# Merging 24 instead of 11 dense blocks behind the last scatter: a predicated copy with its mask in PSUM, and stores from ScalarE's queue

## The chip, the cores and the metric

The kernel runs as one program on one core of a Trainium2 chip. The metric is the device time of one execution in microseconds (us), as the median of some executions. It is a hand-placed program: five engines (TensorE or PE, VectorE or DVE, ScalarE or ACT, GpSimd or POOL, SyncE or SP) each run a list of instructions in a fixed order and meet only at semaphores. SP and ACT can each issue plain DMA transfers from a queue of their own; POOL issues the indirect ones (gathers and scatters by a list of row numbers).

## What is computed

Four graph layers over 100,000 nodes of 64 features, with 25,000 edges. Only nodes that an edge touches get a message. Cut to what matters here:

```python
edge_index = jnp.stack([src, dst])
x = _layernorm(x + _L0_gnn_ref(x, edge_attr_16, src, dst, ...), axis=-1)
x = _layernorm(x + _L1_gnn_ref(x, edge_index, edge_weight, ...), axis=-1)   # attention, layernorm, MLP, layernorm
x = _layernorm(x + _L2_gnn_ref(x, edge_index, ...), axis=-1)
x = _layernorm(x + _L3_gnn_ref(x, src, dst, edge_weight, 100000), axis=-1)
return x                                                                    # (100000, 64) float32
```

A node without edges goes through the same norms and the MLP of layer 1, with constants in place of the messages. That is the dense part. A node with edges needs gathers, softmax and segment sums. That is the sparse part.

## The kernel before

**Dense part.** The 100,000 rows are cut into 98 blocks of 1024 rows (the last one is shifted back to end at row 100,000 and so overlaps the one before). Each block is a chain on PE, ACT and DVE in one of three lanes, and its result, 128 partitions x 512 floats (256 KB), is stored by SP (`dense_sp`). The result is right for the nodes without edges alone.

**Sparse part.** The edges stand in 25 groups of 8 columns of 125. POOL walks five long rows of indirect transfers, 200 each in 25 groups of 8: the gathers of `x` by source and by target, the gathers from `x0tab`, the scatters to `stab`, the gathers from `x2tab` and from `x3tab`. At the end it scatters the final rows of touched nodes to `out`: first 200 of kind "only" (nodes that are targets), then 200 of kind "src". These 400 are the final scatters.

**Why blocks are late.** A dense row of a touched node must not land on top of the scattered one. So POOL waits, ahead of its first final scatter, until every dense block below number `LATE0` is stored in `out`. The last `LATE` blocks (11 of them, numbers 87 to 97) go to a scratch table `late_tab` instead, and may be computed while POOL scatters. Their rows of `out` were filled beforehand with a value that can't be a result, 3e38 (`unset_sp`, on SP). At the end they are merged: once the last scatter has landed, SP loads each late block's rows of `out` (256 KB); a row that still begins with 3e38 was not scattered and takes the dense value, any other keeps the scattered one; then the block is stored. Before, `late_dve` does that with three DVE instructions a block, a mask from the first column and two `tensor_tensor` over 128x512:

```python
nc.vector.tensor_scalar(m, o[:, :, 0], UNSET / 2, UNSET, ALU.is_lt, ALU.mult)   # 3e38 where the row was scattered
nc.vector.tensor_tensor(d, d, bc(m, D), ALU.add)                                # so the dense row becomes huge there
nc.vector.tensor_tensor(o, o, d, ALU.min)                                       # and the smaller one is kept
```

The last block is stored behind all the others, since it overlaps its neighbour.

**What sets the order.** `make_plan` lays all steps of all units out by a greedy list of costs and due times before the program is written, and `play` writes each engine's steps in the order of those times. The late steps (`late_sp`, `late_dve`) have the due time 1e6, so they stand last on their engines. In the plan, the only thing that depends on `LATE` is the row of final scatters, on which nothing else depends. POOL's own list is written in plain loops.

Names in the steps: `late_d` are the dense blocks loaded back from `late_tab`, `late_o` the rows loaded from `out`, `late_m` the masks; `wk` and `u` are large work buffers (`rr` is `u` seen as rows of 136 floats), `b_gl`, `b_h`, `b_s`, `b_x1` the lanes' buffers.

Of the kernel before, what the change touches and what calls it, by code (L numbers as in the profile page):

```python
# [5 lines left out]
i32 = mybir.dt.int32  # L6
# [5 lines left out]
def gnn_resnorm_kernel(nc, x, src, dst, edge_attr, edge_weight, W1, W2, attn, bias0, W_phys, W_neur, att_w,  # L12
# [23 lines left out]
    KEY2 = 0x3F000000 >> 15  # L36
    BIGK, BIGC = 400000.0, 100000.0
    GROUPS = range(NG)
    LATE = 11
    LATE0 = NBLK - LATE  # L40
    UNSET = 3e38
    NONE = 8
# [14 lines left out]
    with ctx:  # L57
# [5 lines left out]
        def S(name):  # L63
            if name not in names:
                names[name] = ctx.enter_context(nc.semaphore(name))
            return names[name]
# [80 lines left out]
        neg2 = sb("neg2", [1, 2])  # L147
        unset = sb("unset", [128, D])
        mask8 = sb("mask8", [128, GC])
        late_d = w_[0:LATE]  # L150
        late_o = [b_gl[k % NL][:, 512 * (k // NL):512 * (k // NL) + 512] for k in range(2 * NL)] + b_h + b_s
        late_m = b_x1[0][:, 0:GC * LATE]
        ps = ctx.enter_context(nc.psum_tensor("ps", [128, 8 * 512], fp32))

        def bank(j, n=1):
            return ps[:, 512 * j:512 * (j + n)]

        pA, pB, pAB = ([bank(2 * l) for l in LANES], [bank(2 * l + 1) for l in LANES], [bank(2 * l, 2) for l in LANES])
        e0, e1 = bank(6), bank(7)

        def col(v, n=128):
            return vec[0:n, v:v + 1]
# [4 lines left out]
        def t3(a, c=GC):  # L167
            return a.rearrange("p (c d) -> p c d", c=c)
# [597 lines left out]
            tab, row = (out, dense_row(n)) if n < LATE0 else (late_tab, NB * (n - LATE0))  # L766
            sp.dma_start(tab[row:row + NB, :].rearrange("(p t) d -> p (t d)", p=128), b_gl[l][:, 0:512]).then_inc(S(f"rows_st{l}"), 16)

        FIRST_FOUND = 6
        LATE_LOADS = [LATE - 1, LATE - 2] + list(range(LATE - 2))  # L770
        LATE_STORES = [LATE - 2] + list(range(LATE - 2)) + [LATE - 1]

        def late_rows(j):
            return out[dense_row(LATE0 + j):dense_row(LATE0 + j) + NB, :].rearrange("(p t) d -> p t d", p=128)

        def unset_sp(sp, t, j):
# [3 lines left out]
                sp.wait_ge(S("late_dma"), 16 * (LATE - 1))  # L780
            sp.dma_start(late_rows(j), unset[:, :].unsqueeze(1).broadcast_to((128, GC, D))).then_inc(S("late_dma"), 16)

        def late_sp(sp, t):
            yield t
            sp.wait_ge(S("summed"), 4 * NG)
            for l in LANES:
                sp.wait_ge(S(f"rows_st{l}"), 16 * before(l, len(lane_jobs[l]), dense=1, src=1))
            sp.wait_ge(S("late_dma"), 16 * LATE)
            for j in range(LATE):
                sp.dma_start(late_d[j], late_tab[NB * j:NB * j + NB, :].rearrange("(p t) d -> p (t d)", p=128)).then_inc(S("late_dma"), 16)  # L790
            sp.wait_ge(S("final_st"), 256 * NG)
            for k, j in enumerate(LATE_LOADS):
                sp.dma_start(t3(late_o[j]), late_rows(j)).then_inc(S(f"late_found{int(k >= FIRST_FOUND)}"), 16)
            sp.wait_ge(S("late_found0"), 16 * FIRST_FOUND)
            for k, j in enumerate(LATE_STORES):
                sp.wait_ge(S("late_step"), 3 * k + 3)
                if k == LATE - 1:
                    sp.wait_ge(S("late_dma"), 32 * LATE + 16 * k)
                sp.dma_start(late_rows(j), t3(late_o[j])).then_inc(S("late_dma"), 16)
            sp.wait_ge(S("late_dma"), 48 * LATE)  # L800

        def late_dve(dve, t):
            yield t
            dve.wait_ge(S("late_dma"), 32 * LATE)
            for k, j in enumerate(LATE_STORES):
                m, d, o = late_m[:, GC * j:GC * j + GC], t3(late_d[j]), t3(late_o[j])
                second = LATE_LOADS.index(j) >= FIRST_FOUND
                dve.wait_ge(S(f"late_found{int(second)}"), 16 * (LATE - FIRST_FOUND if second else FIRST_FOUND))
                nc.vector.tensor_scalar(m, o[:, :, 0], UNSET / 2, UNSET, ALU.is_lt, ALU.mult).then_inc(S("late_step"), 1)  # L809
                dve.wait_ge(S("late_step"), 3 * k + 1)  # L810
                nc.vector.tensor_tensor(d, d, bc(m, D), ALU.add).then_inc(S("late_step"), 1)
                dve.wait_ge(S("late_step"), 3 * k + 2)
                nc.vector.tensor_tensor(o, o, d, ALU.min).then_inc(S("late_step"), 1)

# [246 lines left out]
        def l0_pe(pe, t, g):  # L1063
            yield t["xt"]
            pe.wait_ge(*gathered(0, g))
            pe.wait_ge(S("e0_free"), use("e0", t["xt"]))
            for q in range(Q):
                last_t = nc.tensor.transpose(e0[:, P * q:P * q + P], xs[0:P, GC * g + 2 * q:GC * g + 2 * q + 2, :], ident[0:P, 0:P])
            last_t.then_inc(S("l0_t"), 1)
            yield t["et"]  # L1070
            pe.wait_ge(S(f"ea_in{g % 2}"), 32 * (g // 2 + 1))
            pe.wait_ge(S("e0_free"), use("e0", t["et"]))
            nc.tensor.transpose(e0[:, 0:P], ea_t[g % 2][0:P, :], ident[0:P, 0:P]).then_inc(S("l0_et"), 1)
            yield t["f"]
            pe.wait_ge(S("e0_free"), use("e0", t["et"]) + 1)
            pe.wait_ge(S("e1_free"), use("e1", t["f"]))
            if g == 0:
                pe.wait_ge(S("w_e_in"), 16 * GC)
            nc.tensor.matmul(e1[:, 0:EW], wt[:, W1X, :], e_a[:, 0:EW], start=True, stop=False)
            for q in range(Q):  # L1080
                last_f = nc.tensor.matmul(e1[:, P * q:P * q + P], w_e[:, q, :], e_b[:, 0:P], start=False, stop=(q == Q - 1))
            last_f.then_inc(S("l0_f"), 1)
            yield t["s"]
            pe.wait_ge(S("l0_leaky"), g + 1)
            pe.wait_ge(S("e0_free"), use("e0", t["s"]))
            for q in range(Q):
                last_s = nc.tensor.matmul(e0[0:P, 2 * q:2 * q + 2], e_d[:, P * q:P * q + P], att[:, 0, :], start=True, stop=True)
            last_s.then_inc(S("l0_s"), 1)
# [1249 lines left out]
        def setup_sp(sp):  # L2338
            yield 41
            sp.wait_ge(S("w1e_t"), 1)  # L2340
            for c in range(GC):
                sp.dma_start(w_e[DE * c:DE * c + DE, c // 2, 64 * (c % 2):64 * (c % 2) + 64], w1e_t[0:DE, :]).then_inc(
                    S("w_e_in"), 16)
            yield 44
            sp.wait_ge(S("w_made"), 1)
            sp.dma_start(x0tab[E:E + 128 * NONE, :].rearrange("(p s) d -> p s d", s=NONE),
                         rowc[:, R_B0, :].unsqueeze(1).broadcast_to((128, NONE, D))).then_inc(
                S("x0_none"), 16)

        def signs_dve(dve):  # L2350
            step = [0]
# [16 lines left out]
        @block.sync  # L2368
        def _(sp):
            sp_programs = [index_sp(sp), setup_sp(sp)]  # L2370
            sp_programs += [lists_sp(sp, t0, k, (dlist, slist)[k]) for k, t0 in LISTS]
            sp_programs += lanes(sp, dense_sp, src_sp, dst_sp)
            sp_programs += [l0_sp(sp, at["l0", g], g) for g in GROUPS]
            sp_programs += [prep2_sp(sp, at["prep2", k], k) for k in range(2)]
            sp_programs += [carry_sp(sp, at["lay", layer], layer) for layer in range(4)]
            sp_programs += [edges_sp(sp, n, dlist if n < 2 * NG else slist, t0) for n, t0 in EDGES]
            sp_programs += [main0_sp(sp, n, t0) for n, t0 in MAIN[0]] + [main2_sp(sp, n, t0) for n, t0 in MAIN[1]]
            sp_programs += [rload_sp(sp, at["rl", g], g) for g in GROUPS]
            sp_programs += [unset_sp(sp, at["u3", 0]["t"] + 20 * j, j) for j in range(LATE)]
            sp_programs += [late_sp(sp, 1e6)]  # L2380
            play(*sp_programs)

        @block.gpsimd
        def _(pool):
# [40 lines left out]

            for k in range(2):
                pool.wait_ge(S(f"x0_st{k}"), 32 * ((NG + 1 - k) // 2))
            pool.wait_ge(S("x0_none"), 16)
            pool.wait_ge(S("xd_sum"), NG)
            pool.wait_ge(S("prep2_done"), 1)  # L2430
            pool.sem_inc(S("pool_turn"))
# [37 lines left out]
            for kind, g in FINAL:  # L2469
                pool.wait_ge(S("only_rows" if kind == "only" else "src_rows"), g + 1)  # L2470
                pool.sem_inc(S("pool_turn"))
                for k in range(GC):
                    b = GC * g + k
                    if kind == "src":
                        rows, ix = rsrc[:, b, :], sfin_i
                    else:
                        rows, ix = rdst[:, b, :] if g >= STAGED else staged(g)[:, D * k:D * k + D], fidx_i
                    scatter(out, last_node, ix[:, b:b + 1], rows, S("final_st"))

        @block.tensor  # L2480
        def _(pe):
# [12 lines left out]
        def _(act):  # L2494
# [5 lines left out]
            act_programs += [main_act(act, n, t0) for part in MAIN for n, t0 in part]  # L2500
            act_programs += [xd1_act(act, at["xd1", g], g) for g in GROUPS] + [x1s_act(act, at["x1s", g], g) for g in GROUPS]
            act_programs += [main2_act(act, n, t0) for n, t0 in MAIN[1]] + [main3_act(act, n, t0) for n, t0 in MAIN[2]]
            play(*act_programs)

        @block.vector
# [70 lines left out]
```

## Time and profile before

| | |
|---|---|
| median of 3 runs (lowest to highest) | 2683.65 us (2670.19 to 2685.36) |
| profiled execution: its time, its span | 2680.65 us, 2678.8 us |
| busy: PE, DVE, ACT, POOL | 1807.6, 1724.8, 1465.7, 1679.7 us |
| last scatter issued, last instruction of SP starts | 2649.43 us, 2676.40 us |

The span runs from the first to the last instruction that the profiler recorded; the execution's own time is 1.85 us more. All positions below are in us from the span's start. In rows of the timeline the first number is the start, the second the time from the start of the first to the end of the last of the merged instructions; the bracket is the idle time of the engine ahead of it and what ended that. A DMA issue (SPq, ACTq) is the time on the queue that issues it, not that of the transfer.

### The profile page before, as it was taken

The numbers are of one execution on the slowest core, as the hardware profiler recorded it, in microseconds if no ns is written. First come the engines' busy times: TensorE is split into PE (matmuls) and PEld (weight loads), VectorE is DVE, ScalarE is ACT, GpSimd is POOL, SyncE is SP. The second block draws the span as 40 slices with busy tenths as digits, with TensorE's granted clock in tenths as the row PEclk, the third lists the DMA queues.
The fourth block names the chain that finished last, engine by engine and source line by source line (L and its number), as shares of the span: only waits on it lengthen the run. The fifth ranks groups of instructions, "written<-read, shape, count | busy, mean of one in ns | idle before, by whom it ended". The sixth has DMA issues, their size and how long they took to land. (4 is left out here: it accounts for less than half of the span.)

```text
span 2678.8 us, 24741 instructions
## 1 busy us (share of the span) xinstructions
PE 1807.6 (67%) x7450; PEld 868.5 (32%) x7450; DVE 1724.8 (64%) x3305; ACT 1465.7 (55%) x2212; POOL 1679.7 (63%) x1610
## 2 busy tenths in 40 slices
PE   5999989767977888898999876568877654000000
PEld 3444444324533333344444324433322343000000
DVE  5888989988888787765555469887666775000002
ACT  3787777753676667677777755357777521000000
POOL 5777777710057771006777578775777787777774
PEclk9999999987997888899999986679999755555555
DMA  3333222214622221124444644432121233000002
GB/s 68 73 75 80 68 72 64 63 31 126 192 77 49 60 55 32 47 77 113 138 129 135 179 150 124 117 78 65 58 58 54 86 106 110 16 18 21 22 21 99
DMA packets 236808, 214.81 MB, mean 80 GB/s; under 512 B 157822, under 2 KB 170965, under 8 KB 236677
## 3 DMA queue, kind: packets, MB, share of 16 engines
q1 hardware_dynamic: 182228, 166.60, 21.7%
q0 software_dynamic: 51200, 46.31, 7.2%
q8 instruction: 60, 0.98, 0.2%
q10 hardware_dynamic: 3248, 0.34, 0.1%
q14 instruction: 72, 0.58, 0.1%
HBM read 140.36 MB, written 86.31 MB: 85 GB/s over the span
## 5 line engine op out<-in xcount | busy, mean ns | idle before, releaser
L2405 POOL DMA_INDIRECT stab<-wk,rank_i x200 | 215.0, 1075 | 267.4 <-DVE wk L621 209.1
L578 ACT ACTIVATE b_s<-ps,vec 128x512 f32<-128x512 f32 (+1 forms) x356 | 240.8, 682 | 137.7 <-PE ps L572 45.0
L2402 POOL DMA_INDIRECT e_bc<-x0tab,dpos_i x136 | 137.7, 1013 | 245.7 <-DMA x0tab<-e_bc 200.6
L2402 POOL DMA_INDIRECT u<-x2tab,dpos_i x200 | 227.8, 1139 | 80.2 <-issue 75.3
L809 DVE TENSOR_SCALAR b_x<-b_s 128x8 f32<-128x8 f32 x2 | 0.3, 167 | 396.4 <-DMA b_gl<-out_dram 396.4
L2402 POOL DMA_INDIRECT u<-x3tab,src_i x200 | 206.1, 1030 | 78.8 <-issue 59.4
L2402 POOL DMA_INDIRECT u<-in_x_dram,src_i x200 | 201.7, 1009 | 76.7 <-issue 56.9
L2402 POOL DMA_INDIRECT u<-in_x_dram,dst_i x200 | 207.7, 1038 | 64.3 <-issue 60.9
L2405 POOL DMA_INDIRECT out_dram<-u,sfin_i x200 | 196.5, 982 | 66.3 <-issue 66.3
L2405 POOL DMA_INDIRECT out_dram<-u,dst_i x176 | 197.2, 1120 | 60.6 <-issue 56.0
L566 PE MATMUL ps<-b_h,blk_c 128*128 128x512 f32 (+1 forms) x296 | 169.3, 655 | 35.6 <-ACT b_gl L586 35.1
L561 PE MATMUL ps<-b_h,wt 64*128 64x512 f32 (+1 forms) x296 | 168.4, 654 | 31.4 <-DVE b_x L720 28.5
L1029 PE MATMUL ps<-wk 127*64 127x125 f32 x1200 | 122.1, 370 | 98.3 <-DVE wk L1014 95.0
L572 PE MATMUL ps<-b_s,blk_j 128*128 128x512 f32 (+1 forms) x296 | 158.1, 621 | 34.7 <-ACT b_s L591 34.6
L575 PE MATMUL ps<-b_h,wt 128*128 128x512 f32 (+1 forms) x296 | 165.3, 649 | 15.0 <-DVE b_h L599 14.2
L586 ACT ACTIVATE b_gl<-ps,vec 128x1024 f32<-128x1024 f32 (+1 forms) x148 | 162.7, 1106 | 19.9 <-PE ps L562 18.3
L562 PE MATMUL ps<-b_h,wt 64*128 64x512 f32 (+1 forms) x296 | 168.4, 654 | 0.0
L586 ACT ACT_TABLE_LOAD x124 | 159.1, 1283 | 12.8 <-DMA out_dram<-b_gl 9.3
L567 PE MATMUL ps<-b_gl,w2c 128*64 128x512 f32 (+1 forms) x296 | 163.2, 634 | 0.0
L568 PE MATMUL ps<-b_gl,w2c 128*64 128x512 f32 (+1 forms) x296 | 163.2, 634 | 0.0
L657 PE MATMUL ps<-b_s,blk_j 128*128 128x512 f32 x240 | 136.4, 656 | 19.9 <-ACT b_s L699 11.6
L591 ACT ACTIVATE b_s<-ps,vec 128x512 f32<-128x512 f32 (+1 forms) x148 | 100.5, 679 | 84.4 <-PE ps L568 84.4
(423 smaller groups left out, 4747.4 us busy)
## 6 DMA issues: line engine op xcount, KB each, us to landing
b_gl<-in_x_dram SPq DMA_DIRECT2D x98, 256.0 KB, 2.8
wk<-dlist SPq DMA_DIRECT2D x50, 500.0 KB
wk<-slist SPq DMA_DIRECT2D x50, 500.0 KB
out_dram<-b_gl SPq DMA_DIRECT2D x93, 256.0 KB, 2.0
u<-stab SPq DMA_DIRECT2D x25, 510.0 KB
x2none<-b_gl SPq DMA_DIRECT2D x25, 250.0 KB
x0tab<-e_bc SPq DMA_DIRECT2D x25, 240.0 KB
wk<-x2none SPq DMA_DIRECT2D x25, 240.0 KB
```

Of the source, the lines that this page charges most:

```text
L561: nc.tensor.matmul(pA[l][:, 0:w], wt[0:64, W1T, :], b_h[l][0:64, 0:w], start=True, stop=True)
L562: nc.tensor.matmul(pB[l][:, 0:w], wt[64:128, W1T, :], b_h[l][64:128, 0:w], start=True, stop=True).then_inc(S(f"mlp_pe{l}"), 1)
L566: nc.tensor.matmul(pA[l][:, 0:w], blk_c[:, :], b_h[l][:, 0:w], start=True, stop=False)
L567: nc.tensor.matmul(pA[l][0:64, 0:w], w2c[:, :], b_gl[l][:, 0:w], start=False, stop=True)
L568: nc.tensor.matmul(pA[l][64:128, 0:w], w2c[:, :], b_gl[l][:, 512:512 + w], start=False, stop=True).then_inc(S(f"mlp_pe{l}"), 1)
L572: nc.tensor.matmul(pB[l][:, 0:w], blk_j[:, :], b_s[l][:, 0:w], start=True, stop=True).then_inc(S(f"means{l}"), 1)
L575: nc.tensor.matmul(pA[l][:, 0:w], wt[:, DG2, :], b_h[l][:, 0:w], start=True, stop=True).then_inc(S(f"mlp_pe{l}"), 1)
L578: return nc.scalar.activation(b_s[l][:, 0:w], pB[l][:, 0:w], ACT.Abs_reciprocal_sqrt, bias=col(EPSV))
L586: nc.scalar.activation(b_gl[l][:, :].rearrange("p (b f) -> p b f", b=2)[:, :, 0:w], pAB[l].rearrange("p (b f) -> p b f", b=2)[:, :, 0:w], ...
L657: nc.tensor.matmul(pB[l], blk_j[:, :], b_s[l][:, :], start=True, stop=True).then_inc(S(f"means{l}"), 1)
L2402: pool.indirect_dma_start(out=o, out_offset=None, in_=tab, in_offset=at_ix(ix), **kw).then_inc(s, 16)
L2405: pool.indirect_dma_start(out=tab, out_offset=at_ix(ix), in_=a, in_offset=None, bounds_check=last, oob_is_err=False).then_inc(s, 16)
```

## The change

It makes these edits:

- `LATE` is 24: blocks 74 to 97 are late. 13 more blocks go to `late_tab`, are filled with 3e38 beforehand, are loaded twice and are stored at the end. The fills are due every 12 instead of every 20 us.
- The merge of a block is two DVE instructions: a mask (1 where the first column is still 3e38), written to PSUM, and one `copy_predicated` over 128x512 that copies the dense value onto the loaded rows where the mask is set.
- `late_d` lies in the part of `u` that the "only" scatters read, in pieces of 64 floats. So its 24 loads wait for these 200 scatters, which count on a semaphore of their own (`only_st`). Before, the 11 loads went to `wk` and waited for no scatter.
- The loads of `out` rows go in chunks of three, and each chunk waits for the landing of the chunk two ahead of it (two semaphores in turn). Before, all 11 were issued in a row.
- The stores of merged blocks are issued by ACT (`late_act`) instead of SP.
- The store that fills `x0tab`'s spare rows counts on `w_e_in` instead of on a semaphore of its own; so PE waits for it too ahead of the first `w_e` matmul.

```diff
-    LATE = 11
+    LATE = 24
...
-        late_d = w_[0:LATE]
-        late_o = [b_gl[k % NL][:, 512 * (k // NL):512 * (k // NL) + 512] for k in range(2 * NL)] + b_h + b_s
-        late_m = b_x1[0][:, 0:GC * LATE]
+        late_d = [rr[:, GC * k:GC * k + GC, 0:D] for k in range(LATE)]
+        late_o = [t[:, 512 * k:512 * k + 512] for k in range(2) for t in b_gl] + b_h + b_s + b_x1 + w_
...
+        late_m = bank(0)[:, 0:GC * LATE]
...
-        FIRST_FOUND = 6
+        FOUND = 3
...
+        def late_found(k):
+            c = k // FOUND
+            in_chunk = min(FOUND, LATE - FOUND * c)
+            return S(f"late_found{c % 2}"), 16 * (FOUND * (c // 2) + in_chunk)
...
             sp.wait_ge(S("late_dma"), 16 * LATE)
+            sp.wait_ge(S("only_st"), 128 * NG)
             for j in range(LATE):
-                sp.dma_start(late_d[j], late_tab[NB * j:NB * j + NB, :].rearrange("(p t) d -> p (t d)", p=128)).then_inc(S("late_dma"), 16)
-            sp.wait_ge(S("final_st"), 256 * NG)
+                sp.dma_start(late_d[j], late_tab[NB * j:NB * j + NB, :].rearrange("(p t) d -> p t d", p=128)).then_inc(S("late_dma"), 16)
+            sp.wait_ge(S("final_st"), 128 * NG)
             for k, j in enumerate(LATE_LOADS):
-                sp.dma_start(t3(late_o[j]), late_rows(j)).then_inc(S(f"late_found{int(k >= FIRST_FOUND)}"), 16)
-            sp.wait_ge(S("late_found0"), 16 * FIRST_FOUND)
+                if k % FOUND == 0 and k >= 2 * FOUND:
+                    sp.wait_ge(*late_found(k - 2 * FOUND))
+                sp.dma_start(t3(late_o[j]), late_rows(j)).then_inc(late_found(k)[0], 16)
+
+        def late_act(act, t):
+            yield t
             for k, j in enumerate(LATE_STORES):
-                sp.wait_ge(S("late_step"), 3 * k + 3)
+                act.wait_ge(S("late_step"), 2 * k + 2)
                 if k == LATE - 1:
-                    sp.wait_ge(S("late_dma"), 32 * LATE + 16 * k)
-                sp.dma_start(late_rows(j), t3(late_o[j])).then_inc(S("late_dma"), 16)
-            sp.wait_ge(S("late_dma"), 48 * LATE)
+                    act.wait_ge(S("late_dma"), 32 * LATE + 16 * k)
+                act.dma_start(late_rows(j), t3(late_o[j])).then_inc(S("late_dma"), 16)
+            act.wait_ge(S("late_dma"), 48 * LATE)
...
-                nc.vector.tensor_scalar(m, o[:, :, 0], UNSET / 2, UNSET, ALU.is_lt, ALU.mult).then_inc(S("late_step"), 1)
-                dve.wait_ge(S("late_step"), 3 * k + 1)
-                nc.vector.tensor_tensor(d, d, bc(m, D), ALU.add).then_inc(S("late_step"), 1)
-                dve.wait_ge(S("late_step"), 3 * k + 2)
-                nc.vector.tensor_tensor(o, o, d, ALU.min).then_inc(S("late_step"), 1)
+                m, o = late_m[:, GC * j:GC * j + GC], t3(late_o[j])
+                dve.wait_ge(*late_found(LATE_LOADS.index(j)))
+                if k == 0:
+                    dve.wait_ge(*late_found(0))
+                nc.vector.tensor_scalar(m, o[:, :, 0], UNSET / 2, None, ALU.is_ge).then_inc(S("late_step"), 1)
+                dve.wait_ge(S("late_step"), 2 * k + 1)
+                nc.vector.copy_predicated(o, m.bitcast(i32).unsqueeze(2).broadcast_to((128, GC, D)), late_d[j]).then_inc(
+                    S("late_step"), 1)
...
             if g == 0:
-                pe.wait_ge(S("w_e_in"), 16 * GC)
+                pe.wait_ge(S("w_e_in"), 16 * GC + 16)
...
-            sp_programs += [unset_sp(sp, at["u3", 0]["t"] + 20 * j, j) for j in range(LATE)]
+            sp_programs += [unset_sp(sp, at["u3", 0]["t"] + 12 * j, j) for j in range(LATE)]
...
-                    scatter(out, last_node, ix[:, b:b + 1], rows, S("final_st"))
+                    scatter(out, last_node, ix[:, b:b + 1], rows, S("only_st" if kind == "only" else "final_st"))
...
+            act_programs += [late_act(act, 1e6)]
```

PE's list is the same instruction by instruction. ACT's is the same up to the 24 stores at its end, DVE's up to the merge, POOL's but for the semaphores. What differs stands in the following places.

DVE, the first two blocks of the merge, at the end of its list, before:

```order
L809 TENSOR_SCALAR b_x10<-b_s0 128x8 [waits late_found0,late_dma]
L811 TENSOR_TENSOR wk<-wk,b_x10 128x512 [waits late_step]
L813 TENSOR_TENSOR b_s0<-b_s0,wk 128x512 [waits late_step]
L809 TENSOR_SCALAR b_x10<-b_gl0 128x8 [waits late_found0]
L811 TENSOR_TENSOR wk<-wk,b_x10 128x512 [waits late_step]
L813 TENSOR_TENSOR b_gl0<-b_gl0,wk 128x512 [waits late_step]
```

and after (the first three blocks; `ps` is PSUM):

```order
L820 TENSOR_SCALAR ps<-wk 128x8 [waits late_found0,late_dma]
L822 COPY_PREDICATED wk<-ps,u 128x512 [waits late_step]
L820 TENSOR_SCALAR ps<-b_gl0 128x8 [waits late_found0]
L822 COPY_PREDICATED b_gl0<-ps,u 128x512 [waits late_step]
L820 TENSOR_SCALAR ps<-b_gl1 128x8 [waits late_found1]
L822 COPY_PREDICATED b_gl1<-ps,u 128x512 [waits late_step]
```

Three instructions a block for 11 blocks have become two a block for 24.

SP, its loads and stores at the end of its list, before (from the eighth load on):

```order
L793 DMA b_gl2<-out_0_dram 128x512
L793 DMA b_h0<-out_0_dram 128x512
L793 DMA b_h1<-out_0_dram 128x512
L793 DMA b_h2<-out_0_dram 128x512
L799 DMA out_0_dram<-b_s0 128x512 [waits late_step,late_found0]
L799 DMA out_0_dram<-b_gl0 128x512 [waits late_step]
L799 DMA out_0_dram<-b_gl1 128x512 [waits late_step]
```

and after (the loads from `late_tab`, and the first ten from `out`):

```order
L796 DMA u<-late_tab 128x8x64 [waits rows_st2,late_dma,rows_st1,only_st,rows_st0,summed]
L796 DMA u<-late_tab 128x8x64 x23
L801 DMA wk<-out_0_dram 128x512 [waits final_st]
L801 DMA wk<-out_0_dram 128x512
L801 DMA b_gl0<-out_0_dram 128x512
L801 DMA b_gl1<-out_0_dram 128x512
L801 DMA b_gl2<-out_0_dram 128x512
L801 DMA b_gl0<-out_0_dram 128x512
L801 DMA b_gl1<-out_0_dram 128x512 [waits late_found0]
L801 DMA b_gl2<-out_0_dram 128x512
L801 DMA b_h0<-out_0_dram 128x512
L801 DMA b_h1<-out_0_dram 128x512 [waits late_found1]
```

A chunk's first load now waits for an earlier chunk, and the stores have left this list: they stand at the end of ACT's.

SP during the gathers from `x0tab`, where the fills stand between the dense and `x2none` stores, before:

```order
L781 DMA out_0_dram<-unset 1024x1x64 [waits pool_c]
L767 DMA out_0_dram<-b_gl0 128x512 [waits rows_out0]
L781 DMA out_0_dram<-unset 1024x1x64 [waits pool_c]
L767 DMA out_0_dram<-b_gl1 128x512 [waits rows_out1]
L781 DMA out_0_dram<-unset 1024x1x64 [waits pool_c]
L885 DMA x2none<-b_gl1 125x512 [waits rows_out1]
```

and after:

```order
L767 DMA out_0_dram<-b_gl0 128x512 [waits rows_out0]
L781 DMA out_0_dram<-unset 1024x1x64 [waits pool_c] x2
L767 DMA out_0_dram<-b_gl1 128x512 [waits rows_out1]
L781 DMA out_0_dram<-unset 1024x1x64 [waits pool_c] x2
L895 DMA x2none<-b_gl1 125x512 [waits rows_out1]
```

The stores between which the fills stand keep their order; two fills in a row stand where one stood.

## Rows read from the trace of the kernel before

**Rows 1.** The page, part 4: the chain that ended last, by engine.

```profile
POOL 16%; issue 6%; ACT 4%; DVE 4%; PE 4%; DMA 1%; SPq 0%; POOLq 0%; ACTq 0%; DVEq 0%
```

**Rows 2.** Waits of POOL at the final scatters: us in total, times, longest.

```profile
POOL out_dram L2405 <- issue: 129.7, 399, 3.0
POOL out_dram L2405 <- DVE u L1662: 4.6, 1, 4.6
```

**Rows 3.** Timeline of POOL, last gather and first final scatter.

```profile
2096.40 1.00 POOL L2402 DMA_INDIRECT u<-x3tab,src_i  x1 [0.31 <-issue]
2097.70 1.02 POOL L2405 DMA_INDIRECT out_dram<-e_bc,dst_i  x1 [0.30 <-issue]
```

**Rows 4.** Timeline of SP, last early block's store and first late ones.

```profile
2015.84 0.34 SPq L767 DMA_DIRECT2D out_dram<-b_gl  x1
...
2027.79 6.35 SPq L767 DMA_DIRECT2D late_tab<-b_gl  x2
```

**Rows 5.** Timeline of all engines from the last scatter on.

```profile
2649.43 0.98 POOL L2405 DMA_INDIRECT out_dram<-u,sfin_i  x1 [0.30 <-issue]
2651.62 0.81 SPq L793 DMA_DIRECT2D b_s<-out_dram  x2
...
2658.87 0.17 DVE L809 TENSOR_SCALAR b_x<-b_s 128x8 f32<-128x8 f32 x1 [396.39 <-DMA b_gl<-out_dram]
2659.08 0.69 DVE L811 TENSOR_TENSOR wk<-wk,b_x 128x512 f32<-128x512 f32 x1
2659.80 0.69 DVE L813 TENSOR_TENSOR b_s<-b_s,wk 128x512 f32<-128x512 f32 x1
2660.41 0.17 DVE L809 TENSOR_SCALAR b_x<-b_gl 128x8 f32<-128x8 f32 x1
...
2675.14 0.69 DVE L813 TENSOR_TENSOR b_s<-b_s,wk 128x512 f32<-128x512 f32 x1
2676.40 0.33 SPq L799 DMA_DIRECT2D out_dram<-b_s  x1
```

**Rows 6.** Windows: length, PE, PEld, DVE, ACT, POOL (instructions), PEclk, DMA share, GB/s.

```profile
2652.00:2654.00 2.00, 0.00 (x0) 0.00 (x0) 0.00 (x0) 0.00 (x0) 0.00 (x0) 0.50 0.70 204
2654.00:2656.00 2.00, 0.00 (x0) 0.00 (x0) 0.00 (x0) 0.00 (x0) 0.00 (x0) 0.50 0.81 223
2656.00:2658.00 2.00, 0.00 (x0) 0.00 (x0) 0.00 (x0) 0.00 (x0) 0.00 (x0) 0.50 1.01 381
2658.00:2660.00 2.00, 0.00 (x0) 0.00 (x0) 1.06 (x3) 0.00 (x0) 0.00 (x0) 0.50 1.05 403
...
2666.00:2668.00 2.00, 0.00 (x0) 0.00 (x0) 1.93 (x4) 0.00 (x0) 0.00 (x0) 0.50 0.59 221
```

**Rows 7.** Wait of SP for the other stores, ahead of the last one.

```profile
SPq L798 <- DMA out_dram<-b_h: 1.7, 1, 1.7
```

**Rows 8.** The longest kind of DVE instruction between 2100 and 2260.

```profile
L1014 DVE TENSOR_TENSOR wk<-wk,vcs 127x1000 f32<-127x1000 f32 x25 | 29.7, 1190 | 0.0
```

**Rows 9.** ACT's DMA issues at the start: ns each, min/median/max.

```profile
L2269 ACTq DMA_DIRECT2D vec<-in_L_gnn_ln_g_dram x4: 617/618/618, 15.2 to 18.5; - x4
```

**Rows 10.** Window in the gathers from `x2tab`; columns as in rows 6.

```profile
1540.00:1550.00 10.00, 8.32 (x27) 2.91 (x26) 4.05 (x6) 7.56 (x10) 7.86 (x8) 1.00 0.98 262
```

**Rows 11.** The fills: timeline of one and of a gather behind it.

```profile
752.43 0.61 SPq L781 DMA_DIRECT2D out_dram<-unset  x1
...
757.12 1.35 POOL L2402 DMA_INDIRECT e_bc<-x0tab,dpos_i  x1 [0.30 <-issue]
```

**Rows 12.** Store to `x0tab`'s spare rows, and PE's first matmul of the waiting step.

```profile
37.02 0.62 SPq L2346 DMA_DIRECT2D x0tab<-rowc  x1
...
47.17 1.00 PE L1079 MATMUL ps<-e_a,wt 128*128 128x500 f32 x2
```

**Rows 13.** The page, part 6: DMA issues, KB each, median us to landing.

```profile
out_dram<-unset SPq DMA_DIRECT2D x11, 256.0 KB, 4.9
...
x0tab<-rowc SPq DMA_DIRECT2D x1, 256.0 KB, 3.4
```

More of the change, by code:

```diff
@@ L805, in late_dve @@
             for k, j in enumerate(LATE_STORES):
-                m, d, o = late_m[:, GC * j:GC * j + GC], t3(late_d[j]), t3(late_o[j])
-                second = LATE_LOADS.index(j) >= FIRST_FOUND
-                dve.wait_ge(S(f"late_found{int(second)}"), 16 * (LATE - FIRST_FOUND if second else FIRST_FOUND))
-                nc.vector.tensor_scalar(m, o[:, :, 0], UNSET / 2, UNSET, ALU.is_lt, ALU.mult).then_inc(S("late_step"), 1)
-                dve.wait_ge(S("late_step"), 3 * k + 1)
-                nc.vector.tensor_tensor(d, d, bc(m, D), ALU.add).then_inc(S("late_step"), 1)
-                dve.wait_ge(S("late_step"), 3 * k + 2)
-                nc.vector.tensor_tensor(o, o, d, ALU.min).then_inc(S("late_step"), 1)
+                m, o = late_m[:, GC * j:GC * j + GC], t3(late_o[j])
[6 more added lines that the diff above has]
+                    S("late_step"), 1)
         def src_pe(pe, l, m, t, g):
@@ L2347, in setup_sp @@
                          rowc[:, R_B0, :].unsqueeze(1).broadcast_to((128, NONE, D))).then_inc(
-                S("x0_none"), 16)
+                S("w_e_in"), 16)
         def signs_dve(dve):
@@ L2427, in _ @@
                 pool.wait_ge(S(f"x0_st{k}"), 32 * ((NG + 1 - k) // 2))
-            pool.wait_ge(S("x0_none"), 16)
+            pool.wait_ge(S("w_e_in"), 16 * GC + 16)
             pool.wait_ge(S("xd_sum"), NG)
```

## The prediction

> **What bounds the kernel now.** I read the chain that ended last first. POOL has the largest share of it, and the "issue" beside it is mostly POOL's time between two of its own instructions [rows 1]. Then POOL's waits at the final scatters. The reader is to see that it waits for others only once, 4.6 us for DVE; the other 399 idle pieces are 0.3 us each between two issues, or 3.0 at most [rows 2]. Then the start of this stretch, since that is what late blocks are for. The last gather starts at 2096.40, takes 1.00, and the first final scatter starts at 2097.70, after the usual 0.30 us [rows 3]. So POOL did not wait for a dense block. The store of the last early block had been issued at 2015.84, and the first late one at 2027.79 [rows 4]: block 86 is in `out` some 80 us before POOL asks for it. Last, the tail. The last scatter is issued at 2649.43, the first load at 2651.62, the merge runs on DVE from 2658.87 to 2675.83, the last store is issued at 2676.40 [rows 5], and the span ends at 2678.8. From the last scatter's start that is 29.4 us in which nothing but the merge runs. This tail alone is exposed; everything ahead of it from 2097 on is POOL's row of 400 scatters.
>
> **What 13 more late blocks free: nothing.** PE's list is unchanged, and so are ACT's and DVE's up to the merge; no compute moves. What moves earlier is the point from which POOL may scatter, and POOL waits there 0.30 us, as between any two [rows 3]. The 4.6 us [rows 2] end with a DVE instruction of layer 3, which doesn't depend on dense blocks. So the gain is 0; its upper bound is those 4.6 us.
>
> **The tail, by its DMA.** A block is 0.262 MB. 24 blocks loaded and stored are 24 x 2 x 0.262 = 12.58 MB; before, 11 blocks were 5.77 MB. The loads start slowly: 204 and 223 GB/s in the first four microseconds, so 0.85 MB by 2656 [rows 6]. Then the engines are full: 381 GB/s at a share of 1.01 and 403 at 1.05, so 377 to 384 GB/s at a full share; with stores alone it is 221 at 0.59, or 375 [rows 6]. I take 377 for loads and stores mixed, since both kinds alone give about that. The remaining 11.73 MB then take 31.1 us, until 2687.1. Behind that stands what can't overlap: the last store waits for the landing of all others, 1.7 us [rows 7], and from its issue to the end of the span it is 2678.8 - 2676.40 = 2.4 us [rows 5]; its own 0.7 us of transfer are in the bytes already. So the span would end at 2687.1 + 1.7 + 2.4 - 0.7 = 2690.5, which is **11.7 us later**. The bounds: with 403 GB/s throughout, 29.1 instead of 31.1, so +9.7; at the 262 GB/s that a share of 0.98 moves where gathers with short rows are among the traffic [rows 10], 44.8, so +25.4. The transfers of the tail are 2 KB pieces like those of before, so I stay near the first.
>
> The Trainium skill (DMA: Bandwidth & Descriptors, "Where 436 GB/s comes from") has HBM bind such transfers at about 358 GB/s a core. The row with 403 GB/s speaks against it over two microseconds at least. By that figure the transfers would take 32.8 us and the sum be 1.7 us more.
>
> **DVE in the tail.** Before, a block takes 2659.08 - 2658.87 = 0.21 us for the mask's place, 0.72 for the first `tensor_tensor` and 0.61 for the second [rows 5]; 11 x 1.54 = 16.9. No row shows a `copy_predicated`. If it is like the second `tensor_tensor`, 0.69 busy, a block takes 0.21 + 0.61 = 0.82 and 24 take 19.7 us. Its two bounds: less than 0.69 changes nothing, since the DMA's 31.1 are longer; the longest DVE instruction nearby, 1000 elements, takes 1.19 [rows 8], which makes 0.5 more a block, 31.7 us in all and within 1 us of the DMA. I take 0.69, by the shape. So the cheaper merge is hidden under the transfers; it decides from 31.1 / 24 = 1.3 us a block on.
>
> **ACT's stores.** A DMA issue on ACT took 0.62 us at the start of the kernel [rows 9]: 24 are 14.9 us, beside DVE and DMA, so 0. The queue matters in one way: behind a load that waits for its chunk, SP would hold back stores; on ACT they go as soon as DVE is done. ACT has nothing else left to do, so nobody waits behind them.
>
> **The chunk gate** is an added wait on SP. Queued behind it are only further loads; DVE and ACT wait for those. Before, six loads had landed 2658.87 - 2651.62 = 7.25 us after the first issue [rows 5]. Two chunks are six loads. If six in flight always took 7.25 us, a chunk would pass every 3.6 us, less than the 3.9 us that its 1.57 MB of loads and stores need at 377 GB/s (31.1 / 8). So the gate costs 0 to 2 us, inside the rounding of the sum.
>
> **The loads from `late_tab`** now start only after the 200 "only" scatters. The last 200 scatters at 0.98 + 0.30 us each take some 257 us, so these loads can be issued from about 2392. In the worst case each takes the 4.9 us of a fill, which also moves 256 KB in pieces of 64 floats [rows 13]: 118 us, over before 2520, against a need at 2652. Hidden, 130 us to spare. Do they slow POOL? In a window with DMA at 0.98, POOL still issued 8 gathers in 10 us at 0.98 us each [rows 10]. So 0.
>
> **13 more fills.** They cost SP 0.61 us each [rows 11], 8 us in all on a queue that has gaps there, and put 13 times 0.26 MB more on the DMA. The gather shown behind a fill took 1.35 us [rows 11], against 1.00 for an undisturbed one [rows 3]. If each added fill slowed one gather by 0.35, that would be 4.6 us on POOL, upstream of the end. Whether the fill did it the row doesn't tell, and DMA at 0.98 didn't slow POOL elsewhere [rows 10], so I take 1 us of 0 to 4.6. The last fill waits for the others; behind it on SP stands an `x2none` store that frees a lane, at most one landing, 4.9 us [rows 13], late, and as before.
>
> **The moved semaphore.** PE now waits for the `x0tab` store too. It is issued at 37.02 and lands 3.4 us later [rows 12, 13]; PE starts the step at 47.17 [rows 12]. Six microseconds to spare: 0.
>
> **The sum.** 2680.65 (the profiled execution) + 11.7 + 1 = **2693 us**. The runs shown have a median of 2683.65 and reach from 2670.19 to 2685.36; the profiled one lies 3 us under the median, and a median of three may be off by 5 or so. A change of under 1% (27 us) can't be told from none here, and 12 us is 0.4%.
>
> **Rivals.**
> (a) *Loads and stores don't share a limit*, and the tail goes at DVE's pace. The first chunk lands at about 2656, 19.7 us of DVE follow, then 3.0 us as before from DVE's end to the span's: 2678.7, no change, 2681 us with the fills. For it: stores come from another queue. Against it: it needs 11.7 MB in 20 us, 590 GB/s, and no window passes 403 [rows 6]. Chance 0.10. The Trainium skill (DMA: Bandwidth & Descriptors, "Issuing engines are not separate DMA queues") says that DMAs issued by different engines end up on the same 16; by it, (a) is out and the sum above stands.
> (b) *The chunk gate becomes the bound*, slower than before by over 1%. If stores that alternate with loads double the landing of a window of loads, so that a single chunk passes per 7.25 us, eight chunks take 58 us from 2651.6; three blocks of DVE and the 3.0 us at the end make 2715, so +36, 2717 us. For it: only six loads may be in flight, and the store queue fills as fast as the load queue. Against it: the engines would be idle half the time with work queued, while at 1.01 share they were not. It decides from (2705.6 - 2651.6 - 5.5) / 8 = 6.1 us a chunk. Chance 0.12.
> (c) *`copy_predicated` is twice as dear*, 1.38: 1.51 a block, 36.2 us from 2656, and 3.0: 2695, so 2698 us with the fills. Or the 262 GB/s of above: 2707. Together 0.10.
> (d) *The change does what it is made for*: in other executions POOL does wait for a dense block, and now doesn't. The 80 us between block 86's store and POOL's asking [rows 4] speak against it; a gain of over 1% would need the body to shrink by 39 us. 2654 us. Chance 0.03.
>
> **How the numbers follow.** 0.65 for the forecast with its own range 2687 to 2701. The range goes from 2679, which takes in (a), to 2711, which takes in (c); it leaves out (b) and (d), 0.15. Faster by over 1%: (d), 0.03. Slower by over 1%, past 2710.5: (b) and a corner of (c), 0.14. Within 1%: the rest, 0.83.
>
> **What would show it.** In the changed kernel's profile the first final scatter should stand 0.3 us behind the last gather, at 2097 to 2102; the last scatter at 2649 to 2655; the first `out` load 2.2 us behind it. In the tail the DMA share should be near 1.0 at about 380 GB/s for some 30 us, DVE busy for under two thirds of it and waiting for DMA, and the span's end 40 to 43 us behind the last scatter's start. `copy_predicated` should read 0.6 to 0.8 us. The loads from `late_tab` should be through by 2520 at the latest, with scatters at 0.98 beside them. I am wrong if the share in the tail stays at 0.5 to 0.7 (then the gate or DVE holds it, (b) or (c)), if the windows pass 450 GB/s (then (a)), or if POOL's row begins earlier or runs slower.

## The result, and the profile after

| | before | changed |
|---|---|---|
| median of 20 runs (lowest to highest) | 2682.47 us (2670.19 to 2688.83) | 2687.89 us (2679.70 to 2700.00) |
| ratio to before, 95% interval | | 1.0029 (1.0015 to 1.0042) |
| profiled execution's span | 2678.8 us | 2698.3 us |
| start of the last scatter | 2649.43 | 2658.56 |
| tail: from there to the span's end | 29.4 us | 39.7 us |

The change makes the kernel slower by 0.29%, 7.8 us (4 to 11); the two medians lie 5.4 us apart. The predicted direction holds. Of the forecast 12.7 us, 11.7 were for the tail and 1 for the fills; the tail grew by 10.3, and the whole change lies below the forecast by more than its interval allows. The profiled execution happened to be the slowest of the 20, so its span says less than the ratio; its tail can be read apart from that.

First the place where more late blocks could have helped. POOL's timeline of the changed kernel, last gather and first final scatter, answers to [rows 3]:

```profile
2105.86 1.00 POOL L2412 DMA_INDIRECT u<-x3tab,src_i  x1 [0.30 <-issue]
2107.16 1.02 POOL L2415 DMA_INDIRECT out_dram<-e_bc,dst_i  x1 [0.30 <-issue]
```

The gap is 0.30 us, as it was. Nothing was waited for there before, so nothing was won. Then the tail, the timeline of all engines, to be held against [rows 5]:

```profile
2658.56 0.98 POOL L2415 DMA_INDIRECT out_dram<-u,sfin_i  x1 [0.31 <-issue]
...
2660.75 0.83 SPq L801 DMA_DIRECT2D wk<-out_dram  x2
2661.62 4.84 SPq L801 DMA_DIRECT2D b_gl<-out_dram  x6
2665.76 0.17 DVE L820 TENSOR_SCALAR ps<-wk 128x8 f32<-128x8 f32 x1 [391.55 <-DMA b_gl<-out_dram]
2665.97 0.72 DVE L822 COPY_PREDICATED wk<-ps,u 128x512 f32<-128x512 int32 x1
...
2666.60 0.17 DVE L820 TENSOR_SCALAR ps<-b_gl 128x8 f32<-128x8 f32 x1
2666.73 0.36 ACTq L809 DMA_DIRECT2D out_dram<-wk  x1
...
2679.26 0.17 DVE L820 TENSOR_SCALAR ps<-b_s 128x8 f32<-128x8 f32 x1 [2.15 <-DMA b_x<-out_dram]
...
2683.84 0.17 DVE L820 TENSOR_SCALAR ps<-b_x 128x8 f32<-128x8 f32 x1 [1.98 <-DMA wk<-out_dram]
...
2686.47 9.70 ACTq L809 DMA_DIRECT2D out_dram<-wk  x8
...
2693.75 0.73 DVE L822 COPY_PREDICATED wk<-ps,u 128x512 f32<-128x512 int32 x1
```

A block starts 0.84 us behind the one before it (2666.60 - 2665.76), of which the predicated copy is 0.72. And DVE idles again and again for a load, up to 2.15 us: a reader should look at the brackets, which name a DMA each time. What the DMA did meanwhile is in the windows of the changed kernel (columns as in [rows 6]):

```profile
2662.00:2664.00 2.00, 0.00 (x0) 0.00 (x0) 0.00 (x0) 0.00 (x0) 0.00 (x0) 0.50 0.85 294
2664.00:2666.00 2.00, 0.00 (x0) 0.00 (x0) 0.20 (x2) 0.00 (x0) 0.00 (x0) 0.50 0.82 294
2666.00:2668.00 2.00, 0.00 (x0) 0.00 (x0) 1.79 (x5) 0.00 (x0) 0.00 (x0) 0.50 1.02 334
2668.00:2670.00 2.00, 0.00 (x0) 0.00 (x0) 1.93 (x5) 0.00 (x0) 0.00 (x0) 0.50 0.95 309
2670.00:2672.00 2.00, 0.00 (x0) 0.00 (x0) 1.13 (x4) 0.00 (x0) 0.00 (x0) 0.50 1.04 393
...
2678.00:2680.00 2.00, 0.00 (x0) 0.00 (x0) 0.71 (x2) 0.00 (x0) 0.00 (x0) 0.50 1.05 402
...
2690.00:2692.00 2.00, 0.00 (x0) 0.00 (x0) 1.16 (x4) 0.00 (x0) 0.00 (x0) 0.50 1.06 409
2692.00:2694.00 2.00, 0.00 (x0) 0.00 (x0) 1.90 (x6) 0.00 (x0) 0.00 (x0) 0.50 0.75 283
```

From 2670 to 2692 all engines are full, share 1.04 to 1.06, with loads and stores mixed at 389 to 409 GB/s. Before, the same share was reached for four microseconds [rows 6], and from 2662 on DVE, busy 1.90 to 1.93 of every 2 us, left the DMA at 0.35 to 0.59. Two of those windows of the kernel before:

```profile
2662.00:2664.00 2.00, 0.00 (x0) 0.00 (x0) 1.90 (x6) 0.00 (x0) 0.00 (x0) 0.50 0.42 156
...
2670.00:2672.00 2.00, 0.00 (x0) 0.00 (x0) 1.93 (x4) 0.00 (x0) 0.00 (x0) 0.50 0.35 131
```

The bound of the tail has moved from DVE to the DMA.

The loads from `late_tab`, now beside the "src" scatters. SP's timeline and a window of all engines:

```profile
2400.69 26.17 SPq L796 DMA_DIRECT2D u<-late_tab  x24
```

```profile
2410.00:2420.00 10.00, 0.00 (x0) 0.00 (x0) 0.00 (x0) 0.00 (x0) 7.84 (x8) 0.50 1.29 254
```

POOL issues 8 scatters in these 10 us at 0.98 us each, though the DMA share reads 1.29. From the first "src" scatter's start to the last one's it is 258.8 us, and 261.5 before. So the loads cost nothing.

### The profile page after: what moved, and what is told of

Its sections match the earlier page's. It is cut to its first block and busy times, and to the rows that moved or that the text cites. A ratio compares the mean times of both kernels' runs of the same rounds, so it can differ in the third digit from the quotient of the medians.

```text
span 2698.3 us, 24808 instructions
## 1 busy us (share of the span) xinstructions
PE 1809.6 (67%) x7450; PEld 870.6 (32%) x7450; DVE 1728.6 (64%) x3320; ACT 1467.0 (54%) x2212; POOL 1680.5 (62%) x1610
## 5 line engine op out<-in xcount | busy, mean ns | idle before, releaser
L586 ACT ACT_TABLE_LOAD x124 | 159.1, 1283 | 14.7 <-DMA out_dram<-b_gl 9.2
```

Source lines behind the costliest of these rows:

```text
L586: nc.scalar.activation(b_gl[l][:, :].rearrange("p (b f) -> p b f", b=2)[:, :, 0:w], pAB[l].rearrange("p (b f) -> p b f", b=2)[:, :, 0:w], ...
```

## Experiments

Each is timed against the kernel before, interleaved on one chip: experiments 1 to 4 on one, the others on another, so between these groups ratios are compared and not medians. "Tail" is always from the start of the last scatter to the end of the span, read from one execution of each kernel. Two executions with the tail of the kernel before, that of the result and that of experiment 6, have 29.4 and 29.1 us.

**1. The changed kernel with 11 late blocks.**

```diff
-    LATE = 24
+    LATE = 11
```

> The changed kernel with 11 late blocks instead of 24; the merge with the predicated copy, the chunks of three and ACT's stores stay. Theory A (the tail is paid by its bytes, all beside the last block's store): 5.77 MB, 0.85 of them in the slow start until 4.4 us behind the first load, the rest at the 405 GB/s that the changed kernel's windows show, 12.1 us, then 3.4: from the start of the last scatter to the end 2.2 + 4.4 + 12.1 + 3.4 = 22 us, against 29.4 before and 39.7 in the changed kernel. Against before 7 us faster, ratio 0.997. Rival B (the changed kernel is slower in its body, by the 13 added fills and loads, and the tail's parts cancel): the tail still reads some 29 us and the time is that of before. Rival C (fixed latencies of chunks set the tail): four chunks at 7.25 us, 29 + 5 = 34 us, 5 us slower than before.

Ratio 0.9966 (0.9942 to 0.9989). Its timeline:

```profile
2652.66 0.98 POOL L2415 DMA_INDIRECT out_dram<-u,sfin_i  x1 [0.30 <-issue]
...
2665.75 0.17 DVE L820 TENSOR_SCALAR ps<-b_gl 128x8 f32<-128x8 f32 x1 [1.07 <-DMA b_h<-out_dram]
...
2672.91 0.34 ACTq L809 DMA_DIRECT2D out_dram<-b_s  x1
```

The span ends at 2675.3, so the tail is 22.6 us, against 22 expected, 29.4 before. Theory A holds, B and C fall. So the change is two things of opposite sign: a better way to merge, worth some 7 us at 11 blocks, and 13 blocks more that cost 17 (39.7 - 22.6), or 1.3 us a block. The 7 us belong to three edits together, the predicated copy, the chunks and ACT's stores, which no run takes apart at 11 blocks. The trace shows at least that the chunks matter: the first merge starts 7.4 us behind the last scatter, and 9.4 before, since it waits for three loads instead of six.

**2. Four late blocks.**

```diff
-    LATE = 24
+    LATE = 4
```

> The changed kernel with 4 late blocks. Block 93 is then the last early one; in the trace of before its store was issued at 2089.5 and POOL's first final scatter started at 2097.7. Theory A: POOL still doesn't wait (a gap of 0.3 us ahead of the first final scatter, or at most a few us), and the tail moves 2.1 MB: 2.2 + 4.4 + 3.1 + 3.4 = 13 us; 16 us less than before, ratio 0.994. Rival B (early blocks are needed ahead of the scatters, so more late blocks are worth having): POOL's first final scatter stands behind a wait for a dense store of 10 us or more, and the time is that of before or above.

Ratio 0.9932 (0.9908 to 0.9957), 18 us faster than before (12 to 25). Timelines of POOL and SP around the first final scatter and of the tail's start:

```profile
2090.97 0.33 SPq L767 DMA_DIRECT2D out_dram<-b_gl  x1
...
2097.91 1.02 POOL L2415 DMA_INDIRECT out_dram<-e_bc,dst_i  x1 [0.30 <-issue]
...
2648.23 0.98 POOL L2415 DMA_INDIRECT out_dram<-u,sfin_i  x1 [0.30 <-issue]
```

Block 93 is stored 6.9 us ahead of POOL's first final scatter, and POOL still waits only its 0.30 us. The span ends at 2662.9: a tail of 14.7 us against 13 expected. That is 14.7 us less than before; the other 3 or so of the 18 us lie inside the interval, and no row accounts for them.

**3. No chunk gate.** Here semaphores of earlier stages are used a second time.

```diff
-                if k % FOUND == 0 and k >= 2 * FOUND:
-                    sp.wait_ge(*late_found(k - 2 * FOUND))
...
+            if c < 5:
+                return S(f"x_in{c - 2}"), 16 * before(c - 2, len(lane_jobs[c - 2]), dense=1) + n
+            return ((S("x0_st0"), 32 * ((NG + 1) // 2) + n), (S("x0_st1"), 32 * (NG // 2) + n), (S("x2_st"), 32 * NG + n))[c - 5]
```

> The changed kernel with a semaphore for each chunk of three (eight of them, six that are done with their first use), so that no load waits for an earlier chunk: all 24 are issued in a row. Theory A (the DMA engines are full between the first landing and the last store, share 1.05): the gate costs only the start, where the windows show 0.82 to 1.02; 0 to 2 us gained of the changed kernel's time, DVE never waits after its first block, and stores queue instead. Ratio to before 1.002 to 1.003. Rival B (the gate is the bound): the tail falls from 39.7 us by 5 us or more, ratio 1.001 or below.

Ratio 1.0030 (1.0011 to 1.0049). The tail goes from 2648.58 to 2687.7, 39.1 us, 0.6 less than with the gate. Windows of this kernel:

```profile
2652.00:2656.00 4.00, 0.00 (x0) 0.00 (x0) 0.55 (x2) 0.00 (x0) 0.00 (x0) 0.50 0.98 305
2656.00:2660.00 4.00, 0.00 (x0) 0.00 (x0) 2.92 (x8) 0.00 (x0) 0.00 (x0) 0.50 1.00 341
2660.00:2664.00 4.00, 0.00 (x0) 0.00 (x0) 3.67 (x9) 0.00 (x0) 0.00 (x0) 0.50 1.05 396
```

The share reaches 0.98 at once instead of 0.82 to 0.85, and that is all. One detail was expected wrongly: DVE still waits up to 1.29 us for loads. I read this as loads and stores sharing the engines whether they were queued early or late; no run tests that. The gate is not the bound.

**4. 24 blocks with the old arithmetic** (mask, add, minimum; the operands stay where they are).

```diff
-                nc.vector.tensor_scalar(m, o[:, :, 0], UNSET / 2, None, ALU.is_ge).then_inc(S("late_step"), 1)
-                dve.wait_ge(S("late_step"), 2 * k + 1)
-                nc.vector.copy_predicated(o, m.bitcast(i32).unsqueeze(2).broadcast_to((128, GC, D)), late_d[j]).then_inc(
-                    S("late_step"), 1)
+                nc.vector.tensor_scalar(m, o[:, :, 0], UNSET / 2, UNSET, ALU.is_lt, ALU.mult).then_inc(S("late_step"), 1)
+                dve.wait_ge(S("late_step"), 3 * k + 1)
+                nc.vector.tensor_tensor(d, d, bc(m, D), ALU.add).then_inc(S("late_step"), 1)
+                dve.wait_ge(S("late_step"), 3 * k + 2)
+                nc.vector.tensor_tensor(o, o, d, ALU.min).then_inc(S("late_step"), 1)
```

> The changed kernel with the old merge: mask, add and minimum (three DVE instructions a block, mask in PSUM) instead of mask and predicated copy; all else stays. Theory A: a block takes 1.54 us on DVE instead of 0.83, 24 take 37 us, more than the 29 us of transfers, so DVE becomes the bound: first chunk at 5.0 us behind the first load, 37 us, then 3 us: 2.2 + 5.0 + 37 + 3 = 47 us from the last scatter's start against 39.7, so 7 to 8 us slower than the changed kernel, ratio to before 1.006. DVE is then busy all through the tail and the DMA share falls to 0.8. Rival B (the predicated copy is hidden anyway): the tail stays at 40 us, ratio 1.003.

Ratio 1.0066 (1.0040 to 1.0091), whose interval just touches that of the changed kernel. The tail goes from 2651.76 to 2699.1: 47.3 us, as theory A had it (47). Two of its windows:

```profile
2676.00:2680.00 4.00, 0.00 (x0) 0.00 (x0) 3.83 (x9) 0.00 (x0) 0.00 (x0) 0.50 1.05 406
...
2684.00:2688.00 4.00, 0.00 (x0) 0.00 (x0) 3.83 (x8) 0.00 (x0) 0.00 (x0) 0.50 0.42 156
```

DVE is busy 3.79 to 3.83 of 4 us from 2660 to 2696; the DMA share stays at 0.92 to 1.05 until 2684, where 0.8 was expected, and then falls to 0.42, waiting for DVE to hand it stores. So the predicated copy is worth 7.6 us of tail with 24 blocks, by taking DVE off the bound. A still cheaper merge should be hidden from there on; that was not tested.

**5. The stores on SP's queue,** behind all loads.

```diff
-        def late_act(act, t):
-            yield t
             for k, j in enumerate(LATE_STORES):
-                act.wait_ge(S("late_step"), 2 * k + 2)
+                sp.wait_ge(S("late_step"), 2 * k + 2)
...
-            act_programs += [late_act(act, 1e6)]
```

> The changed kernel with the stores of the merged blocks issued by SP, behind all its loads, instead of by ACT. Theory A (the tail is paid by its bytes, whoever issues them): the 24 loads run alone at some 400 GB/s and take 2.2 + 4.4 + 13.6 us from the last scatter, the stores follow back to back, 6.03 MB at 375 GB/s, 16 us, then 3.4: 40 us, that of the changed kernel (39.7), perhaps 2 more at the seam; ratio to before 1.003 to 1.004. Rival B (it is ACT's queue that lets loads and stores overlap, and the overlap shortens the tail): 45 us or more, ratio 1.005 or above.

Ratio 1.0042 (1.0023 to 1.0061), 0.0013 above the changed kernel, with overlapping intervals. The tail goes from 2655.53 to 2698.1, 42.6 us, 2.9 more. In its windows:

```profile
2664.00:2668.00 4.00, 0.00 (x0) 0.00 (x0) 3.75 (x11) 0.00 (x0) 0.00 (x0) 0.50 0.97 315
...
2676.00:2680.00 4.00, 0.00 (x0) 0.00 (x0) 3.83 (x11) 0.00 (x0) 0.00 (x0) 0.50 0.95 299
2680.00:2684.00 4.00, 0.00 (x0) 0.00 (x0) 3.43 (x9) 0.00 (x0) 0.00 (x0) 0.50 1.05 405
2684.00:2688.00 4.00, 0.00 (x0) 0.00 (x0) 0.19 (x1) 0.00 (x0) 0.00 (x0) 0.50 1.04 396
```

The first store is issued at 2676.55. Until then the engines move loads alone, at 315 to 331 GB/s from 2664 on; the window with the last loads and the first stores has 299, and the stores behind it run at 391 to 405. By theory A's 400 for the loads, they should have been through 3 to 4 us earlier. So the tail lies between the two theories: it is mainly its bytes, as in A, and the overlap that ACT's queue gives is worth some 3 us in the trace. Why the loads are slow here stays open. It is not that loads by themselves must be: in the kernel before, whose first store is issued at 2660.58, loads alone reach 381 and 403 GB/s [rows 6], and mixed windows of the changed kernel read 309 and 334 before 2670.

**6. The added fills by themselves,** in the kernel before: 13 more, into a scratch table that nobody reads.

```diff
+    MORE = 13
...
+    fill_tab = dram("fill_tab", (MORE * NB, D))
...
+            rows = late_rows(j) if j < LATE else fill_tab[NB * (j - LATE):NB * (j - LATE) + NB, :].rearrange("(p t) d -> p t d", p=128)
...
-            sp_programs += [unset_sp(sp, at["u3", 0]["t"] + 20 * j, j) for j in range(LATE)]
+            sp_programs += [unset_sp(sp, at["u3", 0]["t"] + 12 * j, j) for j in range(LATE + MORE)]
```

> The kernel before with 13 more fills of 256 KB, due every 12 us as in the changed kernel, into a scratch table that nobody reads; 11 late blocks and the old merge stay. This is the cost of the added fills by itself. Theory A: 0 to 1 us, ratio 1.000 within its interval, the gathers from x0tab as long as before (269 us). Rival B (each fill slows a gather): 4.6 us or more, ratio 1.002, the gathers 5 us longer.

Ratio 0.9991 (0.9971 to 1.0011). No cost shows, and its interval leaves out more than 3 us, so rival B's 4.6 too; 1 us can't be told from none. The gathers from `x0tab` were not as long as before, though: 272.4 us after 268.8. But their length doesn't follow the number of fills: with 24 fills it was 274.2, 272.3, 269.8, 272.4 and 272.4 us in five kernels, with 11 it was 268.8 and 270.1, with 4 it was 274.6 and 269.8, with 2 it was 272.3.

**7. Two late blocks.**

```diff
-    LATE = 24
+    LATE = 2
```

> The changed kernel with 2 late blocks. Block 95 is then the last early one; in the trace of before its store was issued at 2115.7, when POOL had been scattering for 18 us. Theory A: POOL now waits ahead of its first final scatter, some 20 us until 2118, and the tail is at its fixed part, 12 to 13 us instead of 14.7 with 4 late blocks. Against before that is -18 + 20 - 2 = 0, ratio 1.000; it shows what late blocks are for and that the fourth is the last one worth it. Rival B (the dense chain isn't what holds POOL there, or blocks come earlier in this order): the gap stays under 5 us and the time is that with 4 late blocks or less, ratio 0.993.

Ratio 0.9997 (0.9976 to 1.0017). SP's and POOL's timelines:

```profile
2119.82 0.36 SPq L767 DMA_DIRECT2D out_dram<-b_gl  x1
```

```profile
2092.00 1.00 POOL L2412 DMA_INDIRECT u<-x3tab,src_i  x1 [0.30 <-issue]
2125.40 1.40 POOL L2415 DMA_INDIRECT out_dram<-e_bc,dst_i  x1 [32.40 <-DMA out_dram<-b_gl]
```

Here is the wait that late blocks exist for: 32.4 us, behind the store of block 95 at 2119.82. It is longer than the 20 us expected, since POOL arrived 4.4 us earlier, the store was issued 4.1 us later, and POOL went on 5.6 us behind its issue where some 2 were reckoned. The tail, from 2670.09 to 2681.2, is at 11.1 us. So the gain of the shorter tail is lost at the other end; with 4 blocks POOL doesn't wait there. Three blocks, and five to ten, were not run.

**8. Four late blocks, a semaphore a load, and the last store without its overlap.**

```diff
-    LATE = 24
+    LATE = 4
...
-        FOUND = 3
+        FOUND = 1
...
-            c = k // FOUND
-            in_chunk = min(FOUND, LATE - FOUND * c)
-            return S(f"late_found{c % 2}"), 16 * (FOUND * (c // 2) + in_chunk)
+            if k < 2:
+                return S(f"late_found{k}"), 16
+            return S(f"x_in{k - 2}"), 16 * before(k - 2, len(lane_jobs[k - 2]), dense=1) + 16
...
-                if k % FOUND == 0 and k >= 2 * FOUND:
-                    sp.wait_ge(*late_found(k - 2 * FOUND))
...
-                if k == LATE - 1:
-                    act.wait_ge(S("late_dma"), 32 * LATE + 16 * k)
-                act.dma_start(late_rows(j), t3(late_o[j])).then_inc(S("late_dma"), 16)
+                p = ((NBLK * NB - N) // GC) if k == LATE - 1 else 0
+                act.dma_start(late_rows(j)[p:128], t3(late_o[j])[p:128]).then_inc(S("late_dma"), 16)
```

> The changed kernel with 4 late blocks, a semaphore for each of the 4 loads (so that a block is merged when it has landed and no load waits), and the last block stored without its 44 partitions that overlap its neighbour, so that its store waits for no other. Theory A: the fixed part shrinks by the wait for the other stores, 1.7 us, and by the wait for a whole chunk, 0 to 1: tail 12 to 13 us instead of 14.7, ratio to before 0.992 to 0.993. Rival B: the first merge waits for the two blocks that overlap anyway and the end for the last landing, so nothing is gained: 14.7 us.

Ratio 0.9936 (0.9913 to 0.9960) against 0.9932 of experiment 2. The tail goes from 2651.13 to 2663.6, 12.5 us, 2.2 less than there. In the trace theory A holds; the timing can't tell the two kernels apart. Both beat the kernel before by 17 to 18 us, and by their ratios the changed one by some 25.

## Why the prediction was right

**The gain is nothing.** Right: the gap ahead of the first final scatter is 0.30 us before and after. Experiment 7 shows that the wait is real where late blocks are too few, and experiment 2 that four are enough. Rival (d), a hidden gain, is out.

**The tail is paid by its bytes.** Right in mechanism and nearly in size. The forecast tail was 41.1 us (29.4 + 11.7), the measured one 39.7. The slow start was as taken: in the 4.4 us from the first load's issue the mean is 203 GB/s, 0.9 MB, and in the kernel before 196. The windows of 294 GB/s above only begin later behind the first load than those of [rows 6]. The full rate was taken as 377 GB/s. From there to 2670 it was 335, and then 401 for 22 us, 389 over both together; two errors of opposite sign that leave 0.8 us. That they nearly cancel is luck. From 11 to 24 blocks a block cost 1.3 us (experiment 1), which is its 0.52 MB at 400 GB/s; that, and a DMA share of 1.05 while DVE waits, is the best evidence. Rival (a) needed over 450 GB/s, and no window shown passed 409.

The 358 GB/s that the Trainium skill (DMA: Bandwidth & Descriptors, "Where 436 GB/s comes from") gives for HBM is passed by 22 us on end at 389 to 409, so the measurement decides against it here. The Trainium skill (DMA: Bandwidth & Descriptors, "Issuing engines are not separate DMA queues") says that DMAs of different issuing engines run on the same 16 and interleave. Experiment 5 agrees: the queue moved the tail by 3 us, not by the half that a second set of engines would give.

**The positions were missed.** The first final scatter was to stand at 2097 to 2102 and the last at 2649 to 2655; they stood at 2107.16 and 2658.56. The span's end was to be 40 to 43 us behind the latter, and was 39.7.

**The total.** Of the forecast 12.7 us the tail gave 1.4 less than its share, and the fills' 1 us was not found; the 10.3 left are inside the measured 7.8 (4 to 11), and the rest can't be placed.

**The merge is hidden.** Right: a block takes 0.84 us where 0.82 was forecast, with 0.72 or 0.73 for the copy where 0.69 was taken. DVE was busy 20.0 us in the tail where 19.7 were forecast. Experiment 4 shows the other side: at 1.54 us a block, above the 1.3 from which the prediction said that DVE decides, it does. Rival (c) is out.

**The chunk gate costs 0 to 2 us.** Right: 0.6 us of tail (experiment 3). Rival (b) needed 6.1 us a chunk, and the tail's eight chunks pass at less than 4.

**ACT's stores cost 0.** Right as a cost. The first issue there took 0.36 us, not 0.62, the later ones 0.34 to 1.19. What was missed is the size of a benefit: the prediction saw that stores aren't held back behind loads, but put nothing on it, and experiment 5 has it at some 3 us.

**The fills cost 1 us of 0 to 4.6.** Experiment 6 finds none and leaves out 4.6; whether it is 0 or 1 stays open.

**The loads from `late_tab`** are through in 26 us of issues, far from the bound of 118 us, and don't slow POOL.

**The moved semaphore:** PE started that step at 46.79, 0.4 us earlier than before.

**The 9.1 us by which the last scatter started later** in the profiled execution were not forecast, and no part of the change was found to cause them. 3.4 of them are there at the first gather from `x0tab`, at 756.80 after 753.37, about where the first fill is issued, and 8.8 at the last of these 200 gathers, at 1029.46 after 1020.66. So 5.4 of them arose among the fills, near the 4.6 us that the prediction gave as the fills' worst case; the lengths in experiment 6, which don't follow the number of fills, speak against that cause. The start of the last scatter lay between 2648.2 and 2658.5 in the profiles of the other kernels with 4 or more late blocks, whatever their number, and the ratio over 20 runs (7.8 us) leaves no room for 9 us beside the tail's 10.3. I take it for variation between executions; that is argued from the spread, not shown.

## What to carry to other kernels

Work that is put off behind the last wait is worth it only as far as it shortens that wait: look at the gap where the waiting engine starts first, and if it is at its floor, defer less, not more. Here each deferred block cost 1.1 us of tail from the 4th to the 11th, and 1.3 us from there to the 24th, its 0.52 MB at 400 GB/s. And take a rewritten tail apart: a better mechanism (7 us) and a larger amount (17 us) came in one change, and the time shows only their sum.

## What the hardware showed that was not expected

- The share alone doesn't give the rate, even for transfers of one kind. Loads of 256 KB tiles in 2 KB rows ran at 315 to 331 GB/s at a share of 0.94 to 0.97 in experiment 5, and at 381 and 403 at 1.01 and 1.05 in the kernel before; loads and stores mixed ran at 309 and 334 at first and then at 389 to 409; stores alone at 391 to 396. What sets the slower rate was not found.
- 24 loads of 256 KB in pieces of 256 B took 26 us of issues, with POOL's scatters beside them at 240 to 254 GB/s in all from 2410 to 2430, with a DMA share that reads 1.20 to 1.29. Transfers in 2 KB pieces read 1.05 at 405 GB/s. The share of packet time is thus no measure of how full the engines are across such different pieces.
- A predicated copy of 128x512 floats, with a mask in PSUM that is broadcast along 64 elements, takes 0.73 us, 0.04 more than a `tensor_tensor` of that shape in [rows 5].
